# A four-layer transformer megakernel: rounding moved to GpSimd in the first attention, and the third attention's input rounded per batch inside its main part

## The chip, the cores and the metric

One NeuronCore of a Trainium2 chip runs the whole program in one launch. The metric is the device time of that launch in microseconds (us). On the core, TensorE (PE in the profile; PEld is its weight load) multiplies matrices into PSUM, VectorE (DVE), ScalarE (ACT) and GpSimd (POOL) work elementwise, and SyncE (SP) issues most DMAs. Each engine runs its own instruction list in order; engines wait for each other by semaphores.

## The reference

Activations `x` are 8 batches x 128 tokens x 256 features, the context has the same shape. Each of four layers computes `x = x + attention(layernorm(x), context)` and then `x = x + ffn(layernorm(x))`. The change touches two of the eight parts.

- **First attention (l0)**: 16 heads of 16 features over all 1024 context tokens. Queries, keys and values are rounded to 8 bits, `softmax(q k)` is rounded to 0..255 steps of its row maximum, then multiplied with the values.
- **Third attention (l2)**: the normalised input is scaled by `ln_w`, `ln_b`, divided by one of four per-feature input scales (for q, qx, k, v), clamped to +-448 and rounded to an 8-bit float (3 mantissa bits). Projections give 16 query heads, 16 cross query heads, 8 key heads and 8 value heads of 128 features, and cross keys and values from the context. Queries and keys are layer-normalised per head. Two attentions per batch (self and cross) follow; their outputs, side by side, are divided by `proj_smooth`, clamped and rounded in the same way, and projected back to 256 features by `wproj` (4096 x 256):

```
ln_out = _ln(hidden_states, ln_w, ln_b)
xq     = clip(ln_out / in_scale, -448, 448) -> bf16 -> fp8 e4m3 -> f32      (once per scale)
catq   = the same of concat(core, xout) / proj_smooth
out    = einsum('bsi,oi->bso', catq, wproj) * (proj_in_scale * proj_w_scale)
```

## The kernel before

The eight parts run one after the other, each a block of five engine programs written out by hand; the order of every engine's work is the order in the source.

**`attention_l0`, main part (profile lines 1797 to 1930).** 128 steps, one for each batch and head. In step `n` TensorE writes scores of 128 x 1024 into one of three PSUM buffers (L1817), VectorE takes the row maximum (`top`, L1901), GpSimd turns it into the bias of the exponential (L1807: one multiply-add on 128 x 1), ScalarE computes the exponential with its row sum and stores it as int16, which rounds it (`exps`, L1875), VectorE copies that to bf16 two steps later (`rounding`, L1907), and SyncE transposes it by DMA (L1798). Six steps behind, once in four steps, TensorE multiplies four heads with the values (`value`, L1830, 32 matmuls). Once per batch of 16 steps TensorE also turns the outputs (`turn_back`, `turn_output`) and multiplies them with the output weights (`output`). `score(n)` waits until the exponential of step `n - 3` has read its PSUM buffer.

**`attention_l2`.** It has two blocks.

The first (tiles `l2q_...`, L1256 to L1303) rounds the input for all 1024 tokens before anything else. ScalarE makes `lnT` (two instructions of 128 x 1024) and divides it (eight, L1281); VectorE clamps (L1303) and rounds each by `quantize` (L1220 to L1223: keep the exponent bits, bound the step, add 1.5 * 2^20 steps and take them away again), writing `xq`. Meanwhile SyncE loads `wproj` in 16 pieces into two buffers `wps`, and GpSimd copies each to bf16 (`keep`, L1288).

The second (tiles `l2x_...`, L1305 to L1567) walks over 16 items, two for each batch: side 0 (self) and side 1 (cross). An item has eight steps `t`. `phases(fn)` calls each engine's program with three items at once: `pi` is projected, `ai` (the one before) is in attention, `zi` (before that) finishes. `due(t, lag, ai, zi)` gives the group `a` of four heads (four groups per item) that stands `lag` steps after its start, `norm_due` the projected piece `u` (six per item). What matters here, per step:

- TensorE: projection `t` (L1417, six bf16 matmuls, or L1422), scores at even `t` (L1430), transposes of normalised pieces (L1437), transposes of the probabilities (L1444), values (L1451), and the output projection `y` (L1462) at lag 8.
- ScalarE: copies of the projection (`raw`, L1485), exponentials (L1490), `qT` and `kT` (L1499), `pT` (L1504), the read-out of the attention output into `of` (L1511).
- VectorE: statistics of piece `t` (L1536, `bn`), row maximum at even `t` (L1541), the normalisation of the piece three steps back (L1546, four instructions of 128 x 128), a reciprocal (L1552), and at even `t` clamp and `quantize` of `of` (L1559, L1220 to L1223).
- GpSimd: at `t` = 1, 3, 5 a chain of ten small instructions (L1386 to L1396) that makes the inverse deviations of two pieces, which VectorE's normalisations of steps `t + 2` and `t + 3` wait for; at even `t` the normalisation of the probabilities (L1400, `p_normed`), once VectorE's reciprocal is there.

`Chain.link` issues an instruction and waits for it on its own engine; `Chain.add` only counts it.

Of the kernel before, what the change touches and what calls it, by code (L numbers as in the profile page):

```python
# [1227 lines left out]
def attention_l2(pg, pre):  # L1232
# [8 lines left out]
    with outer:  # L1241
# [3 lines left out]
        xq = ob("xq", [P, 4, KD, T], BF16)  # L1245
        cols, scales = pre.tiles
        lnt, inverse, divided, steps, rounded, wp_kept = (
            pg.sem(f"l2q_{m}") for m in ("ln_affine", "inverse", "divided", "steps", "rounded", "wp_kept"))
        wp_in = [pg.sem(f"l2q_wp_in{i}") for i in range(2)]
        with ExitStack() as st:  # L1250
            def sb(m, shape, dt=F32):
                return st.enter_context(nc.sbuf_tensor(f"l2q_{m}", shape, dt))
            lnT = sb("lnT", [P, KD, T])
            rin = sb("rin", [P, 4 * KD])
            z = sb("z", [P, 2, T], BF16)
            step = sb("step", [P, 2, T], BF16)  # L1256
            wide = sb("wide", [P, 2, T])
            wps = sb("wps", [P, 2, 2, D])
            block = st.enter_context(nc.Block())
            jobs = [(k, j) for k in range(KD) for j in range(4)]  # L1260

            @block.sync
            def _(sp):
                for q in range(16):
                    if q >= 2:
                        sp.wait_ge(wp_kept, q - 1)
                    sp.dma_start(wps[:, q % 2], pg.dram["l2_wp"][:, 2 * q:2 * q + 2, :]).then_inc(wp_in[q % 2], 16)

            @block.scalar
            def _(act):  # L1270
                act.wait_ge(pre.arrived, 32)
                for k in range(KD):
                    nc.scalar.activation(lnT[:, k, :], pg.xnT[:, k, :], ACT.Identity, scale=cols[:, LNW + k:LNW + k + 1],
                                         bias=cols[:, LNB + k:LNB + k + 1]).then_inc(lnt, 1)
                act.wait_ge(inverse, 1)
                act.wait_ge(lnt, KD)
                for n, (k, j) in enumerate(jobs):
                    if n >= 2:
                        act.wait_ge(rounded, n - 1)
                    c = j * KD + k  # L1280
                    nc.scalar.activation(z[:, n % 2], lnT[:, k, :], ACT.Copy, scale=rin[:, c:c + 1]).then_inc(divided, 1)  # L1281

            @block.gpsimd
            def _(pool):

                def keep(q):
                    pool.wait_ge(wp_in[q % 2], 16 * (q // 2) + 16)
                    nc.gpsimd.tensor_copy(wp[:, 2 * q:2 * q + 2, :], wps[:, q % 2]).then_inc(wp_kept, 1)  # L1288
                for n in range(len(jobs)):
                    keep(2 * n)  # L1290
                    keep(2 * n + 1)

            @block.vector
            def _(dve):
                ch = Chain(dve, steps)
                dve.wait_ge(pre.arrived, 32)
                nc.vector.reciprocal(rin[:], cols[:, IN_SCALE:IN_SCALE + 4 * KD]).then_inc(inverse, 1)
                for n, (k, j) in enumerate(jobs):
                    u = n % 2
                    dve.wait_ge(divided, n + 1)  # L1300
                    if n >= 2:
                        dve.wait_ge(rounded, n - 1)
# [6 lines left out]
        with ExitStack() as st:  # L1309
# [3 lines left out]
            def psum(m, shape, dt=F32):  # L1313
                return st.enter_context(nc.psum_tensor(f"l2x_{m}", shape, dt))
# [1052 lines left out]
```

## Time and profile before

| | us |
|---|---|
| median of 3 runs | 1975.74 (1969.93 to 1977.56) |
| the profiled execution: its time | 1987.75 |
| its span | 1986.0 |
| busy: PE, DVE, ACT, POOL | 1622.9, 1170.6, 809.9, 616.7 |
| stage 79 to 302 (first attention, main part) | 223.0 |
| stage 932 to 972 (third attention, first block) | 40.0 |
| stage 972 to 1430 (third attention, main part) | 458.0 |

All times inside the kernel are from that one profiled execution, counted from the start of its span. A group line ends in busy time, mean ns of one instruction, and the idle time of the engine before them with what ended it. A timeline line has start, duration, engine, line and shapes; in square brackets stands how long the engine had been idle and for whom. An instruction that is blocked inside, for a port for example, shows as a longer duration, not as idle time.

### The profile page before, as it was taken

How to read it: one execution, taken by the hardware profiler on the slowest of the kernel's cores; microseconds unless marked ns; L12 is line 12 of the kernel's file. 1: busy time of each engine (PE TensorE's matmuls, PEld its weight loads, DVE VectorE, ACT ScalarE, POOL GpSimd, SP SyncE). 2: the span in 40 equal slices, each digit the busy share in tenths (PEclk: the TensorE clock that was granted, in tenths of full speed). 3: DMA queues.
4: the chain of work that ended last, by engine and by line, in shares of the span. 5: the costliest groups of instructions: out<-in, count | busy, mean ns of one | idle time of the engine just before them, and what ended most of it. 6: DMA issues, size and time to landing. Idle time of an engine off the chain costs nothing. (4 is left out here: it accounts for less than half of the span.)

```text
span 1986.0 us, 25201 instructions
## 1 busy us (share of the span) xinstructions
PE 1622.9 (82%) x8472; PEld 1004.9 (51%) x8472; DVE 1170.6 (59%) x2652; ACT 809.9 (41%) x1871; POOL 616.7 (31%) x980
## 2 busy tenths in 40 slices
PE   6688878999786899995389898898699989737762
PEld 5323234556454455554166666666555565535542
DVE  5799972223554632425789999999822255553225
ACT  3888773111322211112377777777621112412221
POOL 0022211000200197900455555655210000036662
PEclk9755558999687899998699999999889988768886
DMA  2288871110501213111100000000101100245535
GB/s 72 52 161 161 159 149 62 40 40 17 170 1 59 104 59 125 52 52 33 53 1 1 1 1 1 1 1 1 41 20 40 40 23 1 111 156 204 207 126 224
DMA packets 174224, 140.12 MB, mean 71 GB/s; under 512 B 141793, under 2 KB 154721, under 8 KB 170386
## 3 DMA queue, kind: packets, MB, share of 16 engines
q1 hardware_dynamic: 165314, 114.89, 20.6%
q0 software_dynamic: 6416, 22.03, 3.3%
q10 hardware_dynamic: 2368, 1.61, 0.3%
q8 instruction: 69, 1.13, 0.2%
q14 instruction: 57, 0.47, 0.1%
HBM read 85.43 MB, written 19.50 MB: 53 GB/s over the span
## 5 line engine op out<-in xcount | busy, mean ns | idle before, releaser
L1417 PE MATMUL l2x_pr<-l_w,l2x_xq 128*128 128x512 bf16 x576 | 141.1, 383 | 41.0 <-ACT credits L42 40.5
L350 PE MATMUL l1e_gu<-x_normT,l1e_w 128*128 128x512 f32 x384 | 170.8, 599 | 0.0
L1875 ACT ACTIVATE l0m_pf<-l0m_s,l0m_bias,l0x_sq 128x1024 int16<-128x1024 f32 x128 | 154.1, 1204 | 38.9 <-POOL l0m_bias L1807 38.9
L1901 DVE TENSOR_REDUCE l0m_mx<-l0m_s 128x1 f32<-128x1024 f32 x128 | 155.8, 1219 | 21.8 <-PE l0m_s L1817 20.3
L1817 PE MATMUL l0m_s<-l0x_kT,l0x_qT 48*128 48x512 bf16 x256 | 126.1, 620 | 35.9 <-ACT l0m_pf L1875 31.8
L350 PE MATMUL l0e_gu<-x_normT,l0e_w 128*128 128x512 f32 x272 | 121.5, 601 | 0.0
L1807 POOL TENSOR_SCALAR l0m_bias<-l0m_mx,l0x_nsq 128x1 f32<-128x1 f32 x128 | 46.7, 365 | 225.1 <-DVE l0m_mx L1901 222.3
L350 PEld LDWEIGHTS l1e_gu<-x_normT,l1e_w 128*128 128x128 f32 x384 | 73.8, 193 | 83.8 <-issue 82.8
L350 PE MATMUL l2e_gu<-x_normT,l2e_w 128*128 128x512 f32 x256 | 114.4, 602 | 0.0
L1546 DVE TENSOR_SCALAR l2x_raw<-l2x_raw,l2x_mv,l2x_rs 128x128 f32<-128x128 f32 x384 | 111.2, 351 | 3.5 <-POOL l2x_rs L1396 3.3
L1417 PEld LDWEIGHTS l2x_pr<-l_w,l2x_xq 128*128 128x128 bf16 x576 | 56.6, 99 | 96.3 <-ACT credits L42 40.7
L1400 POOL TENSOR_TENSOR x_norm<-x_norm,l2x_rsm 128x512 f32<-128x512 f32 x64 | 74.9, 1171 | 97.2 <-DVE l2x_rsm L1552 97.2
L426 DVE TENSOR_TENSOR l1e_h<-l1e_sil,l1e_gu 128x512 f32<-128x512 f32 x40 | 27.4, 687 | 131.4 <-ACT l1e_sil L402 131.4
L402 ACT ACTIVATE l1e_sil<-l1e_gu 128x512 f32<-128x512 f32 x48 | 28.6, 596 | 179.4 <-PE l1e_gu L350 179.4
L1536 DVE BATCH_NORM_STATS2 l2x_bn<-l2x_raw 128x6 f32<-128x128 f32 x384 | 82.5, 278 | 32.5 <-ACT l2x_raw L1485 32.4
L1437 PE MATMUL l2x_tr<-ident,l2x_raw 128*128 128x128 f32 x384 | 60.5, 280 | 44.6 <-DVE l2x_raw L1546 43.9
L1490 ACT ACTIVATE x_norm<-l2x_s,l2x_mx 128x128 f32<-128x128 f32 x256 | 90.3, 372 | 2.4 <-DVE l2x_mx L1541 2.4
L357 PE MATMUL l1e_y<-l1e_w,l1e_h 128*128 128x256 f32 x384 | 86.3, 379 | 0.6 <-DVE l1e_h L436 0.6
L426 DVE TENSOR_TENSOR l0e_h<-l0e_sil,l0e_gu 128x512 f32<-128x512 f32 x28 | 19.3, 688 | 110.7 <-ACT l0e_sil L402 110.7
L1396 POOL TENSOR_TENSOR l2x_rs<-l2x_rs,l2x_half 128x8 f32<-128x8 f32 x48 | 82.7, 1723 | 3.8
L350 PEld LDWEIGHTS l0e_gu<-x_normT,l0e_w 128*128 128x128 f32 x272 | 52.4, 193 | 60.0 <-issue 59.3
L357 PEld LDWEIGHTS l1e_y<-l1e_w,l1e_h 128*128 128x128 f32 x384 | 72.9, 190 | 19.4 <-issue 9.1
(515 smaller groups left out, 3636.8 us busy)
## 6 DMA issues: line engine op xcount, KB each, us to landing
l3m_w<-in_l_moe SPq DMA_DIRECT2D x16, 1280.0 KB
l1e_w<-in_l_ffn SPq DMA_DIRECT2D x24, 384.0 KB, 3.1
l_rows<-zero_row SPq DMA_DIRECT2D x8, 1024.0 KB, 11.1
l_w<-l_rows SPq DMA_DIRECT2D x8, 1024.0 KB, 11.8
l0e_w<-in_l_ffn SPq DMA_DIRECT2D x17, 384.0 KB, 3.0
l2e_w<-in_l_ffn SPq DMA_DIRECT2D x16, 384.0 KB, 3.1
ctx_tok<-l_route SPq DMA_DIRECT2D x8, 512.0 KB
l2q_wps<-in_l_wp SPq DMA_DIRECT2D x16, 256.0 KB, 2.7
```

The lines of the kernel that those rows point to most:

```text
L350: last = nc.tensor.matmul(gu[half][:, m, :], w[:, c % SW, (2 * k + m) * P:(2 * k + m + 1) * P], pg.xnT[:, k, cols(n)], start=(k == 0), sto ...
L357: last = nc.tensor.matmul(y[:, t, :], h[:, c % SH, t * P:(t + 1) * P], w[:, c % SW, WG:CHUNK], start=(c == 0 and t % 2 == 0), stop=False, ...
L1396: g.tensor_tensor(rs[:, 1, two, :], var, half[:, 0], ALU.pow).then_inc(s["rstd"], 1)
L1400: nc.gpsimd.tensor_tensor(p[:, a % 2], p[:, a % 2], rsm[:, a % 2].unsqueeze(2).to_broadcast([P, U, P]), ALU.mult).then_inc(s["p_normed"], 1)
L1417: last = nc.tensor.matmul(flat(pr[t % 2][:]), src[:, k, tokens], pg.l2_w3[:, part, k, at:at + W], start=(k == 0 and part == 0), stop=(k == ...
L1437: last = nc.tensor.transpose(tr[:, j, :], raw[:, u, j, :], pg.ident[:])
L1490: last = nc.scalar.activation(p[:, a % 2, j, :], s_ps[a % 2][:, j, :], ACT.Exp, bias=mx[:, a % 2, j:j + 1], accum_out=sm[:, a % 2, j:j + 1])
L1536: last = nc.vector.bn_stats(bn[:, t, j, :], raw[:, t, j, :])
L1546: last = nc.vector.tensor_scalar(raw[:, u, j, :], raw[:, u, j, :], mv[:, u, j, 0:1], rs[:, 1, u, j:j + 1], ALU.subtract, ALU.mult)
L1817: last = nc.tensor.matmul(s_ps[n % 3][:, g * HALF:(g + 1) * HALF], qT[:, h, b * P:(b + 1) * P], kT[:, h, g * HALF:(g + 1) * HALF], start=T ...
L1875: nc.scalar.activation(pf[:, n % 4, :], s_ps[n % 3][:], ACT.Exp, scale=sq[:, b, h:h + 1], bias=bias[:, n % 4:n % 4 + 1], accum_out=sm[:, b ...
L1901: nc.vector.tensor_reduce(mx[:, n % 4:n % 4 + 1], s_ps[n % 3][:], AX, ALU.max).then_inc(s["maxed"], 1)
```

## The change

In `attention_l0` GpSimd and VectorE trade two instructions: VectorE makes the bias right behind the maximum (on 128 x 1, after waiting for its own reduction), and GpSimd copies int16 to bf16 (128 x 1024).

In `attention_l2` the first block is gone. `lnT` is kept for the whole part; `xq` holds two batches. Batch 0 is rounded ahead of the main part (four ScalarE instructions of 128 x 128 and one VectorE chain of five instructions on 128 x 512, twice), batch `b + 1` during the two items of batch `b`. The `wproj` pieces are kept in the steps of the first two items, through one buffer. `quantize` loses its last instruction: `widen` ends in the f32 sum, and for `of` the subtraction is GpSimd's at lag 7, with two added waits of GpSimd; `y` moves from lag 8 to lag 9, and `cq` has three buffers. The upper bound of the step (256) goes; 1.5 * 2^20 is multiplied in its place.

```diff
-def quantize(nc, ch, z, step, wide, out):
+def widen(nc, ch, z, step, wide):
     v = nc.vector
     ch.link(v.tensor_scalar(step.bitcast(I16), z.bitcast(I16), 0x7F80, None, ALU.bitwise_and))
-    ch.link(v.tensor_scalar(step, step, 2.0 ** -6, 256.0, ALU.max, ALU.min))
-    ch.link(v.scalar_tensor_tensor(out=wide, in0=step, scalar=1.5 * 2.0 ** 20, in1=z, op0=ALU.mult, op1=ALU.add))
-    return v.scalar_tensor_tensor(out=out, in0=step, scalar=-1.5 * 2.0 ** 20, in1=wide, op0=ALU.mult, op1=ALU.add)
+    ch.link(v.tensor_scalar(step, step, 2.0 ** -6, 1.5 * 2.0 ** 20, ALU.max, ALU.mult))
+    return v.tensor_tensor(wide, step, z, ALU.add)
...
+            @block.sync
+            def _(sp):
+                for q in range(16):
+                    if q >= 1:
+                        sp.wait_ge(wp_kept, q)
+                    sp.dma_start(wps[:], pg.dram["l2_wp"][:, 2 * q:2 * q + 2, :]).then_inc(wp_in, 16)
...
             @block.gpsimd
...
+                def keep(q):
+                    pool.wait_ge(wp_in, 16 * q + 16)
+                    nc.gpsimd.tensor_copy(wp[:, 2 * q:2 * q + 2, :], wps[:]).then_inc(wp_kept, 1)
...
                     for t in range(8):
+                        if job := due(t, 7, ai, zi):
+                            _, a, m = job
+                            pool.wait_ge(s["widened"], m + 3)
+                            if ahead := norm_due(t, 3, pi, ai):
+                                pool.wait_ge(s["normed"], ahead[2] + 1)
+                            nc.gpsimd.tensor_tensor(cq[:, m % 3], wide[:, a % 2], step[:, a % 2], ALU.subtract).then_inc(s["quanted"], 1)
                         if pi is not None and t in (1, 3, 5):
...
                         if job := due(t, 2, ai, zi):
                             _, a, m = job
                             pool.wait_ge(s["recip"], m + 1)
+                            if ahead := due(t, 6, ai, zi):
+                                pool.wait_ge(s["widened"], ahead[2] + 3)
                             nc.gpsimd.tensor_tensor(p[:, a % 2], p[:, a % 2], rsm[:, a % 2].unsqueeze(2).to_broadcast([P, U, P]),
                                                     ALU.mult).then_inc(s["p_normed"], 1)
+                        if pi is not None and pi[0] == 0:
+                            keep(8 * pi[1] + t)
...
             @block.tensor
...
+                            pe.wait_ge(rounded, 2 * pi[0] + 2)
...
-                        if job := due(t, 8, ai, zi):
+                        if job := due(t, 9, ai, zi):
...
                             if side == 0 and a == 0:
+                                pe.wait_ge(wp_kept, 16)
...
             @block.scalar
...
+                def divide(b, half):
+                    act.wait_ge(rounded, 2 * b + half)
+                    for j in range(2):
+                        for k in range(KD):
+                            c = (2 * half + j) * KD + k
+                            nc.scalar.activation(xz[:, j, k, :], lnT[:, k, b * P:(b + 1) * P], ACT.Copy, scale=rin[:, c:c + 1]).then_inc(divided, 1)
...
+                            if t == 1 and pi[0] + 1 < B:
+                                divide(pi[0] + 1, side)
...
             @block.vector
...
+                def clamped(b, half):
+                    ch = xchain(b, half, 0)
+                    dve.wait_ge(divided, 2 * KD * (2 * b + half + 1))
+                    ch.link(nc.vector.tensor_scalar(xz[:], xz[:], 448.0, -448.0, ALU.min, ALU.max))
+                    ch.link(nc.vector.tensor_scalar(xstep[:].bitcast(I16), xz[:].bitcast(I16), 0x7F80, None, ALU.bitwise_and))
+                    ch.add(nc.vector.tensor_scalar(xstep[:], xstep[:], 2.0 ** -6, 1.5 * 2.0 ** 20, ALU.max, ALU.mult))
+
+                def stepped(b, half):
...
+                    ch.add(nc.vector.tensor_tensor(xwide[:], xstep[:], xz[:], ALU.add))
+
+                def narrowed(b, half):
...
+                    nc.vector.tensor_tensor(xq[:, b % 2, 2 * half:2 * half + 2], xwide[:], xstep[:], ALU.subtract).then_inc(rounded, 1)
...
                     for t in range(8):
...
+                        if pi is not None and pi[0] + 1 < B:
+                            if t == 3:
+                                clamped(pi[0] + 1, pi[1])
+                            if t == 5:
+                                stepped(pi[0] + 1, pi[1])
+                            if t == 7:
+                                narrowed(pi[0] + 1, pi[1])
...
@@ -1800,12 +1830,10 @@
             def _(pool):
                 for n in range(N):
-                    b, h = divmod(n, H)
-                    pool.wait_ge(s["maxed"], n + 1)
-                    if n >= 4:
-                        pool.wait_ge(s["exped"], n - 3)
-                    nc.gpsimd.tensor_scalar(bias[:, n % 4:n % 4 + 1], mx[:, n % 4:n % 4 + 1], nsq[:, b, h:h + 1], float(np.log(255.0)),
-                                            ALU.mult, ALU.add).then_inc(s["biased"], 1)
+                    pool.wait_ge(s["exped"], n + 1)
+                    if n >= 8:
+                        pool.wait_ge(moved[n % 8], 16 * (n // 8))
+                    nc.gpsimd.tensor_copy(pi[:, n % 8, :], pf[:, n % 4, :]).then_inc(s["rounded"], 1)
...
                     nc.vector.tensor_reduce(mx[:, n % 4:n % 4 + 1], s_ps[n % 3][:], AX, ALU.max).then_inc(s["maxed"], 1)
-
-                def rounding(n):
...
+                    dve.wait_ge(s["maxed"], n + 1)
+                    if n >= 4:
+                        dve.wait_ge(s["exped"], n - 3)
+                    nc.vector.tensor_scalar(bias[:, n % 4:n % 4 + 1], mx[:, n % 4:n % 4 + 1], nsq[:, b, h:h + 1], float(np.log(255.0)),
+                                            ALU.mult, ALU.add).then_inc(s["biased"], 1)
```

## Rows read from the trace of the kernel before

**Rows 1.** Windows view: stretch, busy of each engine, clock, DMA share, GB/s.
```profile
972.00:1430.00 458.00, 404.09 (x2368) 281.85 (x2368) 410.68 (x1231) 337.38 (x1062) 246.87 (x548) 1.00 0.00 1
```

**Rows 2.** Timeline, first attention: start, duration, engine, line.
```profile
119.82 1.23 DVE L1901 TENSOR_REDUCE l0m_mx<-l0m_s 128x1 f32<-128x1024 f32 x1 [0.47 <-PE l0m_s L1817]
121.14 0.37 POOL L1807 TENSOR_SCALAR l0m_bias<-l0m_mx,l0x_nsq 128x1 f32<-128x1 f32 x1 [2.36 <-DVE l0m_mx L1901]
121.55 1.20 ACT L1875 ACTIVATE l0m_pf<-l0m_s,l0m_bias,l0x_sq 128x1024 int16<-128x1024 f32 x1 [1.43 <-POOL l0m_bias L1807]
...
131.33 1.23 DVE L1901 TENSOR_REDUCE l0m_mx<-l0m_s 128x1 f32<-128x1024 f32 x1 [0.32 <-PE l0m_s L1817]
...
132.95 1.20 ACT L1875 ACTIVATE l0m_pf<-l0m_s,l0m_bias,l0x_sq 128x1024 int16<-128x1024 f32 x1 [0.47 <-POOL l0m_bias L1807]
...
134.30 1.03 PE L1817 MATMUL l0m_s<-l0x_kT,l0x_qT 48*128 48x512 bf16 x2 [0.21 <-ACT l0m_pf L1875]
...
137.30 1.04 PE L1830 MATMUL l0m_o<-l0m_pT,l0x_v 128*32 128x128 bf16 x32
138.28 2.02 PE L1817 MATMUL l0m_s<-l0x_kT,l0x_qT 48*128 48x512 bf16 x4
139.35 1.23 DVE L1901 TENSOR_REDUCE l0m_mx<-l0m_s 128x1 f32<-128x1024 f32 x1
...
157.99 1.23 DVE L1901 TENSOR_REDUCE l0m_mx<-l0m_s 128x1 f32<-128x1024 f32 x1 [0.32 <-PE l0m_s L1817]
```

**Rows 3.** Tile views: durations min/median/max in ns, first and last start.
```profile
L1907 DVE CAST l0m_pi<-l0m_pf x128: 412/416/427, 83.3 to 291.0; 128x1024 bf16<-128x1024 int16 x128
L74 POOL CAST l_w<-l_raw x36: 1037/1038/1456, 700.8 to 844.9; 128x1024 bf16<-128x1024 f32 x36
```

**Rows 4.** Timeline, second attention: a tiny VectorE instruction beside a GpSimd one.
```profile
506.88 3.52 POOL L781 MEMSET l1x_vz<- 128x4096 f32 x1
506.97 3.44 DVE L879 TENSOR_SCALAR l1x_own<-l1x_quarter 128x2 f32<-128x2 f32 x1 [2.97 <-POOL l1x_nm L780]
```

**Rows 5.** Tile views, the block that goes, and the first main instruction.
```profile
L1281 ACT ACTIVATE l2q_z<-l2q_lnT,l2q_rin x8: 1133/1148/1149, 934.9 to 964.1; 128x1024 bf16<-128x1024 f32 x8
L1288 POOL CAST l2x_wp<-l2q_wps x16: 616/676/1597, 935.2 to 962.3; 128x512 bf16<-128x512 f32 x16
...
DMA to landing us min/median/max: 2.5/2.7/3.5
...
972.13 0.13 PEld L1417 LDWEIGHTS l2x_pr<-l_w,l2x_xq 128*128 128x128 bf16 x2 [40.75 <-ACT credits L42]
```

**Rows 6.** Tile views, third attention's main part: durations.
```profile
L1220 DVE TENSOR_SCALAR l2x_step<-l2x_z x64: 293/294/1014, 1012.4 to 1426.9; 128x512 int16<-128x512 int16 x64
L1223 DVE SCALAR_TENSOR_TENSOR l2x_cq<-l2x_step,ctx_tok x64: 691/692/1411, 1014.5 to 1428.2; 128x512 bf16<-128x512 bf16 x64
L1400 POOL TENSOR_TENSOR x_norm<-x_norm,l2x_rsm x64: 1035/1132/1378, 1001.6 to 1420.5; 128x512 f32<-128x512 f32 x64
```

**Rows 7.** Timeline, third attention: starts of items, then one link of its loop.
```profile
1023.77 0.21 POOL L1386 TENSOR_TENSOR l2x_rs<-l2x_bn 128x8 f32<-128x8 f32 x1 [2.79 <-DVE l2x_bn L1536]
...
1155.74 0.87 DVE L1536 BATCH_NORM_STATS2 l2x_bn<-l2x_raw 128x6 f32<-128x128 f32 x4 [1.35 <-ACT l2x_raw L1485]
...
1180.74 1.10 DVE L1546 TENSOR_SCALAR l2x_raw<-l2x_raw,l2x_mv,l2x_rs 128x128 f32<-128x128 f32 x4
...
1183.62 0.87 DVE L1536 BATCH_NORM_STATS2 l2x_bn<-l2x_raw 128x6 f32<-128x128 f32 x4 [1.38 <-ACT l2x_raw L1485]
...
1192.66 2.09 POOL L1396 TENSOR_TENSOR l2x_rs<-l2x_rs,l2x_half 128x8 f32<-128x8 f32 x1
1194.72 1.04 POOL L1400 TENSOR_TENSOR x_norm<-x_norm,l2x_rsm 128x512 f32<-128x512 f32 x1
1194.79 1.82 DVE L1546 TENSOR_SCALAR l2x_raw<-l2x_raw,l2x_mv,l2x_rs 128x128 f32<-128x128 f32 x4
...
1197.94 1.64 POOL L1396 TENSOR_TENSOR l2x_rs<-l2x_rs,l2x_half 128x8 f32<-128x8 f32 x1
```

More of the change, by code:

```diff
@@ L1244, in attention_l2 @@
         wp = ob("wp", [P, 32, D], BF16)
-        xq = ob("xq", [P, 4, KD, T], BF16)
+        lnT = ob("lnT", [P, KD, T])
+        xq = ob("xq", [P, 2, 4, KD, P], BF16)
         cols, scales = pre.tiles
-        lnt, inverse, divided, steps, rounded, wp_kept = (
+        lnt, inverse, divided, xsteps, rounded, wp_kept = (
             pg.sem(f"l2q_{m}") for m in ("ln_affine", "inverse", "divided", "steps", "rounded", "wp_kept"))
[L1249 to L1302, printed above, removed]
-                    ch.link(nc.vector.tensor_scalar(z[:, u], z[:, u], 448.0, -448.0, ALU.min, ALU.max))
-                    quantize(nc, ch, z[:, u], step[:, u], wide[:, u], xq[:, j, k, :]).then_inc(rounded, 1)
@@ L1412, in fn @@
                             if side == 0 or 2 <= t < 6:
-                                src = xq[:, (K_, K_, Q_, Q_, Q_, Q_, V_, V_)[t] if side == 0 else QX]
+                                src = xq[:, pi[0] % 2, (K_, K_, Q_, Q_, Q_, Q_, V_, V_)[t] if side == 0 else QX]
                                 at = t * W if side == 0 else 4096 + (t - 2) * W
@@ L1461, in fn @@
                                 first, final = side == 0 and a == 0 and j == 0, side == 1 and a == 3 and j == U - 1
-                                last = nc.tensor.matmul(y[:, 0:D], cq[:, a % 2, j, :], wp[:, side * 16 + a * U + j, :], start=first, stop=final)
+                                last = nc.tensor.matmul(y[:, 0:D], cq[:, m % 3, j, :], wp[:, side * 16 + a * U + j, :], start=first, stop=final)
                             if side == 1 and a == 3:
@@ L1518, in _, with xchain @@
                 pg.credit(nc.vector, s["quanted"], 2)
+                pg.credit(nc.vector, s["widened"], 2)
+                XSTEPS = 4
+                def xchain(b, half, n):
+                    ch = Chain(dve, xsteps)
+                    ch.base, ch.n = (2 * b + half) * XSTEPS, n
+                    return ch
+                def clamped(b, half):
[5 more added lines that the diff above has]
+                def stepped(b, half):
+                    ch = xchain(b, half, 3)
+                    ch.wait()
+                    ch.add(nc.vector.tensor_tensor(xwide[:], xstep[:], xz[:], ALU.add))
+                def narrowed(b, half):
+                    xchain(b, half, XSTEPS).wait()
+                    if b >= 2:
+                        dve.wait_ge(s["proj"], 16 * (b - 1))
+                    nc.vector.tensor_tensor(xq[:, b % 2, 2 * half:2 * half + 2], xwide[:], xstep[:], ALU.subtract).then_inc(rounded, 1)
+                dve.wait_ge(pre.arrived, 32)
+                nc.vector.reciprocal(rin[:], cols[:, IN_SCALE:IN_SCALE + 4 * KD]).then_inc(inverse, 1)
+                for half in range(2):
+                    clamped(0, half)
+                    stepped(0, half)
+                    narrowed(0, half)
                 for c in range(4):
@@ L1897, in top @@
                 def top(n):
+                    b, h = divmod(n, H)
                     dve.wait_ge(s["scores"], n + 1)
```

44 lines of the change are left out of this document (29 added, 15 removed).

## The prediction

> **What bounds the kernel now.** I read the stages first (windows view and tiles' first and last starts), because the parts run one after another and only two of them change. Outside them nothing moves, so everything below is about 223 us of the first attention's main part, the 40 us block of the third attention and its main part of 458 us [rows 1].
>
> In the first attention the timeline shows what ends each wait. A loop runs over three steps: an exponential starts at 132.95, the scores that take its buffer start at 134.30 (1.35 later); scores at 138.28 give a maximum at 139.35 (1.07); a maximum at 119.82 gives the bias at 121.14 (1.32) and the exponential at 121.55 (0.41) [rows 2]. Sum 4.15, or 1.38 a step. TensorE inserts work into it in order: the value matmuls push the next scores by 0.98 (137.30 to 138.28), once in four steps. One scores-pair costs TensorE 0.83 more of its own, so four steps cost 4.15 + 0.98 + 0.83 = 5.96, and a batch of 16 four of those plus the turns and the output projection. Maxima 16 steps apart stand 26.66 apart (131.33 and 157.99) [rows 2]. VectorE (1.22 for the maximum, 0.42 for the copy, overlapping to 1.47 a step) is right behind it [rows 2, 3].
>
> In the third attention's main part VectorE is busy 410.7 of 458 us, TensorE 404.1, ScalarE 337.4, GpSimd 246.9, at full granted clock [rows 1]; an item takes 27.9 us (1155.74 to 1183.62) [rows 7]. VectorE's durations spread: the same mask instruction takes 0.29 or 1.01, the last rounding step 0.69 or 1.41; GpSimd's p_normed takes 1.04 to 1.38 [rows 6]. And when p_normed (1194.72, 1.04) starts right after a chain, the four normalisations behind that chain take 1.82 instead of 1.10 [rows 7]. So a wide GpSimd instruction and most VectorE instructions exclude each other, and one of them waits for the whole of the other.
>
> **The change, part by part (in terms of the profiled execution).**
>
> *First attention.* The bias moves to VectorE. No row shows it on 128 x 1 there; I take 0.17 (a lower end of 0.1 and an upper one of 0.37, GpSimd's own row). Maximum to exponential falls from 1.73 to about 1.5, the loop by 0.23. VectorE per step: 1.22 + 0.03 + 0.09 = 1.34, below 1.47, so it does not take over. A batch holds four loop passages: 4 x 0.23 = 0.92 us, 8 batches: 7.4; I take -8. The copy on GpSimd is bounded by its cast of 128 x 1024 (f32 to bf16) with 1.04 to 1.46 [rows 3]; the source here is int16. At 1.04 it fits into a step of 1.6 and ends earlier than VectorE's did, which came two steps late. At 1.46 it still fits.
> The trace speaks against this part in one place: a VectorE tensor_scalar of 128 x 2 stood 3.44 us beside a GpSimd memset of 3.52 [rows 4]. If 128 x 1 behaves like it, the bias can wait up to a whole copy (1.04). It fits between two copies while ScalarE runs without a gap; after each delay of TensorE by 0.2 to 1.2 it does not, and is put off until the copy ends. That is some five times in a batch, 2.8 us, less the 0.9 won: +15 over 8 batches (a range of 0 to +30). The Trainium skill, "Vector Engine (DVE) Microarchitecture Reference", section 5.1 (Performance modes), lets a one-source instruction take both ports, the second of them shared with GpSimd, when its outermost dimension above one is even, or odd and equal in source and destination. The row with two elements agrees; whether one element on each side counts as odd and equal (the +15) or as no such dimension at all (the -8) the page leaves open, and no row here shows it.
>
> *First block of the third attention: removed.* Projections began at 972.13 [rows 5], the block at 932. Now: lnT of batch 0 (0.6), four divisions (1.2, from 1.15 for 128 x 1024), one VectorE chain 0.3 + 0.33 + 0.33 + 0.65 + 0.7, then the second four and the chain again, since `divide(0, 1)` waits for `rounded`: about 9 us. Projections from 941: -31.
>
> *`keep` in the first two items.* One buffer: copy (0.62), issue, landing (2.7) [rows 5] is 3.4 us per piece, and GpSimd waits for it in order, with the chains and p_normed behind. A pair of steps with a chain costs 3.9 (chain) + 0.62 + 2.8 + 0.62 = 8.0, as one landing is hidden by the chain and the other is not; the pair without chain 6.9. Laid out from 941 the first chain of item 2 starts at 1007.9 instead of 1023.77 [rows 7]. So of the 31 us 16 remain; bounds: landing 2.5 gives 18, copies of 1.6 beside VectorE 8. SyncE's queue holds nothing else. TensorE's first y waits for all 16 pieces; the last is kept at 1004.9, before that y is due (step 1 of item 2), so this wait costs nothing.
>
> *Items 2 to 13.* VectorE loses per group one 0.69 instruction (4 per item, -2.9), gains per item 0.3 + 0.33 + 0.33 + 0.65 + 0.65 = 2.3. GpSimd gains four subtractions, with mixed inputs about 1.05 as p_normed [rows 6]. ScalarE gains four small divisions (1.2), inside its idle quarter. By busy time all have room. But VectorE and GpSimd now pass work to and fro. From the end of the chain of `t` = 1 (time 0):
> - p_normed follows at once and blocks the normalisation of `t` = 3, which ends at 1.85 (1194.75 to 1196.61 in rows 7). The clamp of `clamped` takes the port next (2.15), then the subtraction (3.2), which the mask waits for. Chain of `t` = 3, 3.85 long: 7.05.
> - VectorE: mask and bound 3.8, statistics, maximum, normalisation, reciprocal 6.3, clamp and widen 1.75: 8.05. Only then p_normed of `t` = 4 (added wait): 9.15. Normalisation of `t` = 5: 10.1; `stepped` 10.8; subtraction 11.9; chain of `t` = 5: 15.8. p_normed of `t` = 6 follows at once and blocks the normalisation of `t` = 7: 17.6.
> - From there into a side 1: `narrowed` 0.65, statistics 0.8, maximum 0.6, normalisation 1.0, reciprocal 0.1, widen 1.75, p_normed 1.1, subtraction 1.05, chain 3.95: 11.0. Into a side 0 the projection has to wait for `narrowed`, then 1.4 + 0.7 until the statistics: 13.1.
> Two items: 2 x 17.6 + 11.0 + 13.1 = 59.3, or 29.65 each, against 27.8: +1.85, over 12 items +22. If every exclusion falls well (0.8 less at `t` = 3 and at `t` = 7, no clamp between) it is 27.8: 0; if the chains are slowed to 4.5 by VectorE's instructions, 31.3: +42. I take +22. TensorE (25 us of work per item) and the y matmuls, a step later with a third buffer, are covered by it; uncovered, TensorE's end of an item would not fall below 25.
>
> *The last two items and the drain.* No input rounding; groups cost VectorE 2.4 instead of 3.1 to 3.8, and ScalarE (3.2 a group) comes next; one subtraction more at the very end: -5.
>
> Sum: -8 - 31 + 15 + 22 - 5 = -7 (the 16 above is 31 - 15). The profiled execution took 1987.75, 12 above the median; I carry the difference to the median: 1975.7 - 6 = 1970.
>
> **Rivals.**
> A. *GpSimd's steps fall between VectorE's as placed, and the item stays at 27.8 or falls a little.* For: VectorE's blocked time in the rows (0.7 on one of its instructions in most groups) is about 2 us an item, and the added waits aim at just that. Against: the path above counts GpSimd at 20.5 us of work per item plus 9 of waits. Time: 1970 - 22 = 1948.
> B. *The bias instruction waits for GpSimd's copy.* It decides once a bias is issued while a copy runs. For: rows 4. Against: one element. -8 becomes +15: 1970 + 23 = 1993, slower.
> C. *The loop between VectorE and GpSimd costs more*, because VectorE's instructions also hold up the chain's small ones: +3.5 an item, 1970 + 20 = 1990, slower. For: one chain's last instruction took 2.09, another's 1.64 [rows 7].
> D. *The copy on GpSimd does not do what the cast row says*: int16 input above 1.6 us makes GpSimd the bound of 128 steps; at 2.0 it is +45: 2020. Against: both rows of casts and their even spread.
>
> **How the numbers follow.** Forecast 0.36, A 0.32, B 0.18, C 0.10, D 0.04. Half a per cent is 10 us, about what a measurement can tell. The forecast's own range is 1958 to 1982, with 0.07 of its chance below 1966 and 0.03 above 1985.6. A is faster but for 0.01; B, C and D are slower but for 0.01. Faster 0.07 + 0.31 = 0.38, same 0.26 + 0.02 = 0.28, slower 0.03 + 0.31 = 0.34. The range 1938 to 1996 leaves out D, the lower edge of A and the upper edges of B and C, some 2 in 10.
>
> **What would show it.** First attention: maxima 16 steps apart 25.7 instead of 26.66, the bias on VectorE near 0.17 (B: a spread up to 1.2), GpSimd's copy near 1.04. First projection near 941. Item 2's first chain near 1008, with GpSimd idle for the `wps` DMAs some 30 us in all. Items 29.7 us apart (A: 27 to 28; C: above 31), the normalisation behind the chains of `t` = 1 and `t` = 5 at 1.8. GpSimd waiting for VectorE's widened, normed about 9 us an item. The prediction is wrong if items are shorter than 28.5, if the keeps do not stretch items 0 and 1, or if the copy is above 1.5.

## The result, and where the time went

The changed kernel took 2007.74 us (median of 4 runs, 2004.56 to 2008.85) against 1976.65 us before (4 runs, 1969.93 to 1979.67): a ratio of 1.0175, 95% interval [1.0151, 1.0199], so it is slower by 1.5 to 2%. 1970 had been forecast, and a range up to 1996.

The profiled execution has a span of 2006.8 us, against 1986.0 before. This difference of 20.8 understates the 31 us between the medians: the last expert part, which is the same code in both, took 271.2 us in the profile of before and 258.9 in the one of after. So stages are compared and not spans. The first attention's main part went from 223.2 to 217.1 us. The third attention, from its first instruction to its last y matmul, ended 1429.6 us into the span before and 1464.6 after: +35.0, of which the table gives the parts (starts of items are the first statistics of each; items are numbered from 0, and items with an odd number are side 1).

| third attention, us | before | after | difference |
|---|---|---|---|
| start of item 2 | 1017.2 | 1001.75 | -15.45 |
| items 2 to 13, mean of one | 27.73 | 31.43 | +3.70 (x 12 = +44.4) |
| start of item 14 to the last y matmul | 79.7 | 85.7 | +6.0 |

Counted from the first instruction of the third attention (932.36 before, 930.90 after) item 2 starts 14.0 earlier; 1.5 of the -15.45 belongs to what stands ahead of that part.

The first attention behaves as the loop of [rows 2] said. Timeline of the changed kernel, the same place (start, duration, engine, line):

```profile
134.20 1.23 DVE L1930 TENSOR_REDUCE l0m_mx<-l0m_s 128x1 f32<-128x1024 f32 x1
...
135.12 1.04 POOL L1836 CAST l0m_pi<-l0m_pf 128x1024 bf16<-128x1024 int16 x1 [0.87 <-ACT l0m_pf L1903]
135.46 0.21 DVE L1934 TENSOR_SCALAR l0m_bias<-l0m_mx,l0x_nsq 128x1 f32<-128x1 f32 x1
...
135.71 1.20 ACT L1903 ACTIVATE l0m_pf<-l0m_s,l0m_bias,l0x_sq 128x1024 int16<-128x1024 f32 x1 [0.65 <-DVE l0m_bias L1934]
```

Its tile views (min/median/max in ns) answer to [rows 3] and [rows 4]:

```profile
L1934 DVE TENSOR_SCALAR l0m_bias<-l0m_mx,l0x_nsq x128: 212/214/215, 83.7 to 286.0; 128x1 f32<-128x1 f32 x128
...
L1836 POOL CAST l0m_pi<-l0m_pf x128: 1037/1042/1045, 85.3 to 287.6; 128x1024 bf16<-128x1024 int16 x128
```

From the start of the maximum to the exponential it is 1.51 us (1.73 before), and the bias of 135.46 runs in the middle of a copy. The spread is what one reads in the tile views: 212 to 215 ns in all 128 cases, of which 29 lie wholly inside a copy; and no copy takes more than 1045. An instruction that had waited for the other engine would show it as length, as the 3.44 us of [rows 4] did. Maxima 16 steps apart stand 25.88 us apart in most batches, where 26.66 was the figure before.

The start of the third attention came as worked out. Timeline and tile view of the changed kernel; the first row answers to 972.13 in [rows 5], the second is the staged copy, the third the DMA it waits for:

```profile
940.16 0.13 PEld L1384 LDWEIGHTS l2x_pr<-l_w,l2x_xq 128*128 128x128 bf16 x2 [10.39 <-DVE l2x_xq L1534]
```

```profile
L1326 POOL CAST l2x_wp<-l2x_wps x16: 603/612/734, 933.7 to 1002.4; 128x512 bf16<-128x512 f32 x16
its engine sat idle before it (us, times) until:
  DMA l2x_wps<-in_l_wp: 23.4, 10
```

The loss is in the items. The stage's windows row against [rows 1] says first what it is not: VectorE's busy time fell from 410.7 to 396.1 us, and yet the stage is longer. TensorE is busy 425.9 of 525, at a granted clock of 0.96.

```profile
940.00:1465.00 525.00, 425.93 (x2330) 290.08 (x2368) 396.11 (x1237) 361.00 (x1113) 328.35 (x623) 0.96 0.03 8
```

The groups of the page name the waits (busy, mean ns | idle before, and what ended it):

```profile
L1384 PE MATMUL l2x_pr<-l_w,l2x_xq 128*128 128x512 bf16 x538 | 140.4, 398 | 39.8 <-DVE l2x_xq L1534 36.4
...
L1558 DVE BATCH_NORM_STATS2 l2x_bn<-l2x_raw 128x6 f32<-128x128 f32 x384 | 83.1, 278 | 73.6 <-ACT l2x_raw L1474 73.6
...
L1364 POOL TENSOR_TENSOR x_norm<-x_norm,l2x_rsm 128x512 f32<-128x512 f32 x64 | 66.6, 1041 | 103.7 <-DVE ctx_tok L1218 103.7
```

TensorE now waits 36.4 us for `xq`, the rounded input, eight times: 10.39 at the start of the part, and seven times 3.15 to 3.93 where a new batch begins (26 together). VectorE's statistics wait 73.6 us for the raw projections that come late behind that (32.4 before). GpSimd's normalisation waits 103.7 us for VectorE's `widen`, a wait that the change put there; but before it had stood idle at the same place for 97.2 us, for VectorE's reciprocal, so its idle time alone does not tell what the new wait costs. One passage from a side 1 into a side 0 shows how the first comes about (timeline of the changed kernel):

```profile
1119.49 1.64 POOL L1358 TENSOR_TENSOR l2x_rs<-l2x_rs,l2x_half 128x8 f32<-128x8 f32 x1
...
1121.09 1.04 POOL L1364 TENSOR_TENSOR x_norm<-x_norm,l2x_rsm 128x512 f32<-128x512 f32 x1
1121.16 1.82 DVE L1568 TENSOR_SCALAR l2x_raw<-l2x_raw,l2x_mv,l2x_rs 128x128 f32<-128x128 f32 x4 [1.81 <-POOL l2x_rs L1358]
1122.91 0.68 DVE L1534 TENSOR_TENSOR l2x_xq<-l2x_xwide,l2x_xstep 128x512 bf16<-128x512 f32 x1
...
1123.64 0.98 PEld L1384 LDWEIGHTS l2x_pr<-l_w,l2x_xq 128*128 128x128 bf16 x6 [3.81 <-DVE l2x_xq L1534]
1123.87 1.24 PE L1384 MATMUL l2x_pr<-l_w,l2x_xq 128*128 128x512 bf16 x5 [3.76 <-DVE l2x_xq L1534]
...
1125.15 0.69 ACT L1474 ACTIVATE l2x_raw<-l2x_pr,l2c_scales 128x512 f32<-128x512 f32 x1 [3.04 <-PE l2x_pr L1384]
...
1125.87 0.87 DVE L1558 BATCH_NORM_STATS2 l2x_bn<-l2x_raw 128x6 f32<-128x128 f32 x4 [1.89 <-ACT l2x_raw L1474]
```

`narrowed` stands last in VectorE's item, behind a normalisation that waits for GpSimd's chain and then for GpSimd's p_normed (1.82 instead of 1.10). TensorE's first projection of the next batch asks for it: TensorE stands still for 3.76 us, and being in order it does none of its other work meanwhile.

The stop has a second price, in TensorE's clock. Two pairs of items of the changed kernel (items 5 and 6, items 9 and 10):

```profile
1093.78:1155.54 61.76, 50.63 (x293) 34.64 (x297) 49.39 (x156) 45.32 (x140) 40.20 (x77) 1.00 0.01 1
1218.92:1283.55 64.63, 53.14 (x293) 36.72 (x297) 49.58 (x156) 45.33 (x140) 40.19 (x77) 0.95 0.00 1
```

At five of the seven stops (those that end at 998.70, 1185.61, 1249.17, 1313.81 and 1376.72) the granted clock falls to the lower of its two levels, 1.2 GHz, within 1.5 us of the stop's end; at the two that end at 1062.11 and 1123.87 it does not. The pairs of items without a low stretch take 61.75 us each, and items 2 to 13 take 377.2 where six such pairs would take 370.5. Some 6 of these 6.7 us lie in items 7 to 13, which have the low stretches: about 0.5 an item.

### The profile page after: what moved, and what is told of

Same layout as the page of the kernel before. It is cut to its first block and busy times, and to the rows that moved or that the text cites. A ratio compares the mean times of both kernels' runs of the same rounds, so it can differ in the third digit from the quotient of the medians.

```text
span 2006.8 us, 25491 instructions
## 1 busy us (share of the span) xinstructions
PE 1640.5 (82%) x8434; PEld 1012.7 (50%) x8472; DVE 1109.7 (55%) x2629; ACT 828.9 (41%) x1929; POOL 771.1 (38%) x1044
## 5 line engine op out<-in xcount | busy, mean ns | idle before, releaser
L1836 POOL CAST l0m_pi<-l0m_pf 128x1024 bf16<-128x1024 int16 x128 | 133.4, 1042 | 137.0 <-ACT l0m_pf L1903 136.1
L1384 PE MATMUL l2x_pr<-l_w,l2x_xq 128*128 128x512 bf16 x538 | 140.4, 398 | 39.8 <-DVE l2x_xq L1534 36.4
L1568 DVE TENSOR_SCALAR l2x_raw<-l2x_raw,l2x_mv,l2x_rs 128x128 f32<-128x128 f32 x384 | 130.4, 399 | 35.9 <-POOL l2x_rs L1358 35.9
L1558 DVE BATCH_NORM_STATS2 l2x_bn<-l2x_raw 128x6 f32<-128x128 f32 x384 | 83.1, 278 | 73.6 <-ACT l2x_raw L1474 73.6
L1404 PE MATMUL l2x_tr<-ident,l2x_raw 128*128 128x128 f32 x384 | 65.4, 296 | 58.4 <-DVE l2x_raw L1568 58.4
L1364 POOL TENSOR_TENSOR x_norm<-x_norm,l2x_rsm 128x512 f32<-128x512 f32 x64 | 66.6, 1041 | 103.7 <-DVE ctx_tok L1218 103.7
L1339 POOL TENSOR_TENSOR l2x_cq<-ctx_tok,l2x_step 128x512 bf16<-128x512 f32 x64 | 81.9, 1280 | 45.2 <-DVE l2x_raw L1568 41.8
L1404 PEld LDWEIGHTS l2x_tr<-ident,l2x_raw 128*128 128x128 f32 x384 | 46.2, 149 | 89.0 <-DVE l2x_raw L1568 85.1
```

Of the source, the lines that this page charges most:

```text
L1339: nc.gpsimd.tensor_tensor(cq[:, m % 3], wide[:, a % 2], step[:, a % 2], ALU.subtract).then_inc(s["quanted"], 1)
L1384: last = nc.tensor.matmul(flat(pr[t % 2][:]), src[:, k, :], pg.l2_w3[:, part, k, at:at + W], start=(k == 0 and part == 0), stop=(k == KD - ...
L1404: last = nc.tensor.transpose(tr[:, j, :], raw[:, u, j, :], pg.ident[:])
L1558: last = nc.vector.bn_stats(bn[:, t, j, :], raw[:, t, j, :])
L1568: last = nc.vector.tensor_scalar(raw[:, u, j, :], raw[:, u, j, :], mv[:, u, j, 0:1], rs[:, 1, u, j:j + 1], ALU.subtract, ALU.mult)
L1836: nc.gpsimd.tensor_copy(pi[:, n % 8, :], pf[:, n % 4, :]).then_inc(s["rounded"], 1)
```

## The experiments

Three theories stood at the start. H: passing work to and fro between VectorE and GpSimd costs what the item gained. W: the two waits that place GpSimd's wide steps cost it. X: the rounding of the input inside the items costs it. Where a run's ratio is given, it is to the kernel before on the same chip. The changed kernel, the runs up to no_x, the next four and the last four were timed in separate groups, so ratios are compared between groups and not times; each ratio is known to 0.0015 to 0.003, 3 to 6 us.

**l0_only.** The kernel before with the first attention's trade alone (lines 1807 and 1907 of before: bias to VectorE, copy to GpSimd).

> The kernel before with the first attention's trade alone (bias on VectorE, copy on GpSimd). The two traces show batches of 25.88 instead of 26.66 us, the bias at 0.21 us without a spread and the copy at 1.04, so this should give -5 to -6 us: 1971. If the trade has side effects on the parts behind it, or the trace's 6 us is the chance of one execution, it is 0.

Ratio 0.9962 [0.9947, 0.9978], 1981.43 us on a chip where before took 1988.81; first attention 216.2 us, items of the third 27.70. So the trade is a gain of some 7 us, in the size of the prediction's -8 and a little over the 5 to 6 expected here, and the loss sits elsewhere.

**no_waits.**

```diff
-                            if ahead := norm_due(t, 3, pi, ai):
-                                pool.wait_ge(s["normed"], ahead[2] + 1)
...
-                            if ahead := due(t, 6, ai, zi):
-                                pool.wait_ge(s["widened"], ahead[2] + 3)
```

> The changed kernel without the two added waits of GpSimd that only place its wide steps (normed before the subtraction, widened before p_normed). Theory W, the placing waits themselves are the cost: items fall from 31.5 to about 28.5 us, 2008 - 40 = 1968. Theory H, the hand-over between VectorE and GpSimd costs it with or without the placing, since either engine then waits for the port: VectorE's blocked instructions come back (some 0.7 us per group), items 30.5 to 31, about -10: 1998. Theory X, the input rounding inside the items is the cost: no change, 2005 to 2008.

Ratio 1.0065 [1.0045, 1.0085]; items 30.60, and the tail behind item 14 80.6 instead of 85.7. W is worth 0.011, about 22 us, by the timed ratios, and 14 us by the profiles of the part; the 40 us expected if W were all are missed, so that is not all.

**sub_dve.** As no_waits, and the subtraction is VectorE's again, right behind `widen`:

```diff
-                            nc.gpsimd.tensor_tensor(cq[:, m % 3], wide[:, a % 2], step[:, a % 2], ALU.subtract).then_inc(s["quanted"], 1)
...
+                            nc.vector.tensor_tensor(cq[:, m % 3], wide[:, a % 2], step[:, a % 2], ALU.subtract).then_inc(s["quanted"], 1)
```

> The changed kernel with the subtraction of the outputs back on VectorE behind widen (0.69 us each, four an item) and without the placing waits; the input rounding stays in the items. H: GpSimd is light again, the loop through it is gone; VectorE has the 27.7 of before plus 2.3 of input rounding: items of 29 to 30 us, 1975 to 1985. W: like the kernel without waits or slightly slower. X: stays at 31 or more, 2005.

Ratio 1.0117 [1.0086, 1.0149]; items 31.18, 0.6 more than in no_waits. H falls: the 29 to 30 that it expected are missed, and GpSimd's subtraction is a gain here. The gate does not hide the answer, since TensorE's stop there is 2.53 us in this run and 2.66 in no_waits. split_nw_ld below says the same: there the work is still passed to and fro, and the items are only 0.42 longer than before.

**no_x.** The input of batches 1 to 7 isn't rounded; TensorE reads batch 0's.

```diff
-                            pe.wait_ge(rounded, 2 * pi[0] + 2)
+                            pe.wait_ge(rounded, 2)
...
-                                divide(pi[0] + 1, side)
...
-                                clamped(pi[0] + 1, pi[1])
...
-                                stepped(pi[0] + 1, pi[1])
...
-                                narrowed(pi[0] + 1, pi[1])
```

> The changed kernel with the input rounding of batches 1 to 7 left out (they use batch 0's rounded input, so the output of those batches is not the reference's); GpSimd's subtraction and both waits stay. X: items fall to 27.7 or below, 2008 - 50 = 1958. H: the loop between VectorE and GpSimd stays, without the clamp and mask at t = 3 (-1.8) and narrowed at t = 7 (-0.7, and -1.5 where a side 0 follows): items of 28.5 to 29, 1970. W: 29 to 30, 1980.

Ratio 0.9927 [0.9904, 0.9951]; items 28.16. X is the main cause: 3.3 of the 3.7 us an item hang on it, though both placing waits are in. (From item 3 on the granted clock is 1.00 in this run, so the clock's 0.5 an item is in the 3.3.) A second reading matters as much. Windows view of this kernel's stage, as [rows 1]:

```profile
937.00:1418.00 481.00, 417.78 (x2368) 285.05 (x2365) 370.33 (x1159) 339.43 (x1057) 332.84 (x623) 0.98 0.03 9
```

VectorE is busy 40 us less than in [rows 1], some 2.5 an item, and the item is not shorter than before's 27.73. The placing waits are still in this run. If they cost here what they cost in split_nw (0.9 an item), the item without them would be about 27.3, an estimate: at most 0.5 us won for 2.5 us of VectorE's time. So VectorE's busy time was hardly what set the item of before.

X itself can work in three ways, which the next four runs are to separate: G, TensorE waits for `xq`; S, ScalarE's four divides (1.27 us together) hold up the exponentials and the next raw copy; D, VectorE's added work stretches the chain.

**late_divide.** `divide` moved from behind the raw copy of `t` = 1 to the end of `t` = 2.

> The changed kernel, but ScalarE's four divides of the next batch stand at the end of t = 2 of an item, behind the raw copies of the second group and the copy of the attention's output, and not between raw and exp at t = 1 (4 x 0.39 = 1.6 us an item). Run with three others (early_narrow, ungated, no_divide) that split the 3.4 us an item which leaving the rounding out gave back. Theory S (ScalarE's divides hold up exp and the second raw, which the normalising chain waits for): items at 31.5 - 1.5 = 30.0 us, ratio to before about 1.008. Theory G (TensorE's projection of the next batch waits for the rounded input): the divides come later, so the gate opens no earlier; 31.5 or more, ratio 1.017 to 1.022. Theory D (VectorE's and GpSimd's own added work stretches the chain): no change, 1.017.

Ratio 1.0123 [1.01, 1.0145]; items 30.62.

**no_divide.** `divide` left out after batch 0.

> ScalarE's divides of batches 1 to 7 left out, everything else as in the changed kernel: VectorE rounds what batch 0's divides left. Theory S: items at 31.5 - 1.6 = 29.9, ratio 1.007. Theory G: little, since narrowing stays at its place: 1.015. Theory D (work on VectorE and GpSimd): 1.017. Against late_divide it tells whether moving the divides gives all that removing them gives.

Ratio 1.0131 [1.0102, 1.016]; items 30.60. Moving the divides gives just what leaving them out gives: 0.8 us an item. It is their place that costs, not their time. S holds, but for a minor part (30.0 and 29.9 had been expected if it were all). In both runs TensorE still stops at the gate, 3.52 us per batch, and late_divide's odd items 3 to 13 have clocks of 0.95 or 0.96, so the 0.8 is not measured at full clock.

**early_narrow.**

```diff
-                            if t == 7:
+                            if t == 6:
                                 narrowed(pi[0] + 1, pi[1])
```

> The changed kernel, but VectorE's narrowing of the rounded input stands at t = 6 and not at t = 7. Theory G: TensorE's idle in front of the projection's first transposes (36 us of 39.8 in the changed kernel) falls by up to 4.5 us for eight items: ratio down by 0.010 to 0.018, to 1.000 to 1.008. Theory S: nothing or little, 1.015 to 1.018. Theory D: 1.017, or worse by the 0.68 us of the narrowing now in front of the last reading of the chain.

Ratio 1.0056 [1.0038, 1.0074]; items 29.87. One line moved by one step gives back 0.012. TensorE's stop is 0.82 us at the first new batch and at most 0.24 at the later ones, and the granted clock is 1.00 in items 2 to 13. G is the main part.

**ungated.** All rounding is done (its results for batches 1 to 7 all go to the second buffer); TensorE reads batch 0's and waits for no later one:

```diff
-                            pe.wait_ge(rounded, 2 * pi[0] + 2)
+                            pe.wait_ge(rounded, 2)
...
-                                src = xq[:, pi[0] % 2, (K_, K_, Q_, Q_, Q_, Q_, V_, V_)[t] if side == 0 else QX]
+                                src = xq[:, 0, (K_, K_, Q_, Q_, Q_, Q_, V_, V_)[t] if side == 0 else QX]
```

> All the rounding of the input is done, at its places, but TensorE always reads batch 0's rounded input and waits for no later one; the projections of batches 1 to 7 thus come from batch 0's rows. Theory G: nearly all of the 3.4 us an item comes back, items at 28.3, ratio about 0.995. Theory S: the divides still hold up the second raw; items at 31, ratio 1.015. Theory D: no change, 1.017. If it lands between (items at 29.9), the gate is worth what comes back and the work the rest.

Ratio 1.0035 [1.0021, 1.005]; items 29.57, between the 28.3 expected if G were all and the 31 expected if S were. The gate is worth 0.014, its effect on the clock included; what is left against no_x (28.16) is 1.4 an item for the work itself.

This suggests a repair. K and Q, needed at once, do not have to wait for V and for side 1's Q: round them as the first half, an item earlier.

**split_gate.**

```diff
-                            pe.wait_ge(rounded, 2 * pi[0] + 2)
+                            pe.wait_ge(rounded, 2 * pi[0] + (1 if side == 0 and t < 6 else 2))
...
-                            c = (2 * half + j) * KD + k
+                            c = (half + 2 * j) * KD + k
...
-                    nc.vector.tensor_tensor(xq[:, b % 2, 2 * half:2 * half + 2], xwide[:], xstep[:], ALU.subtract).then_inc(rounded, 1)
+                    nc.vector.tensor_tensor(xq[:, b % 2, half::2], xwide[:], xstep[:], ALU.subtract).then_inc(rounded, 1)
```

> The changed kernel, but the input is rounded in another pairing: the first half is the one that K and Q read, the second the one that QX and V read, and TensorE waits at side 0's first six projections for the first half alone, which is narrowed an item earlier. Nothing else is moved. Theory G (what early_narrow and ungated point to: TensorE waits for the half narrowed at the end of the item before): items like ungated's, 29.5 us, ratio 1.002 to 1.005. If the delay came from VectorE's added work in front of the chain's small ones and not from the gate: 1.012 to 1.018.

Ratio 1.0032 [1.0013, 1.005]; items 29.64, as in ungated. The whole cost of the gate was an order of data, at no cost in work. The granted clock is 1.00 from item 2 to item 13. Items 5 and 6 take 58.99 us together, against 61.76 in the changed kernel at the same clock: the stop itself is worth 1.4 an item, and the clock's 0.5 comes on top in the items that had it. The first projection also needs one half only: it comes 5.5 us after the part's first instruction and not 9.3.

**split_nw.** split_gate and no_waits together.

> split_gate without the two waits that place GpSimd's subtraction and normalisation behind VectorE's. If the gate's and the waits' costs add (0.014 and 0.011 of the time): ratio 0.992. If the waits cost only because they delayed the gate: no better than split_gate, 1.003. Items at 28.6 us if they add, 29.5 if not.

Ratio 0.9926 [0.9903, 0.9949], 1955.56 us against 1969.32; items 28.73, tail 80.0. The two costs add. Here the waits are worth 0.0106 by the timed ratios and 16 us (0.008) by the profiles. The same passage as above, timeline of this kernel:

```profile
1103.34 1.41 POOL L1360 TENSOR_TENSOR x_norm<-x_norm,l2x_rsm 128x512 f32<-128x512 f32 x1
...
1103.77 2.69 DVE L1564 TENSOR_SCALAR l2x_raw<-l2x_raw,l2x_mv,l2x_rs 128x128 f32<-128x128 f32 x4
...
1104.18 1.07 PEld L1380 LDWEIGHTS l2x_pr<-l_w,l2x_xq 128*128 128x128 bf16 x6
...
1104.29 1.46 PE L1380 MATMUL l2x_pr<-l_w,l2x_xq 128*128 128x512 bf16 x6
...
1104.72 1.15 POOL L1337 TENSOR_TENSOR l2x_cq<-ctx_tok,l2x_step 128x512 bf16<-128x512 f32 x1
```

The normalisation takes 2.69 us here, behind both wide GpSimd steps, against 1.82 in the changed kernel: the exclusion is worse. But TensorE's projection starts without a wait, 2.1 us before VectorE writes the other half of `xq`. The page's groups:

```profile
L1380 PE MATMUL l2x_pr<-l_w,l2x_xq 128*128 128x512 bf16 x576 | 143.4, 387 | 7.7 <-DVE l2x_xq L1530 6.3
...
L1360 POOL TENSOR_TENSOR x_norm<-x_norm,l2x_rsm 128x512 f32<-128x512 f32 x64 | 77.5, 1210 | 56.4 <-DVE l2x_rsm L1570 55.6
```

p_normed takes 1210 ns on average without its placing wait and 1041 with it (in split_gate as in the changed kernel); and the kernel with the shorter one is the slower. Which of the instructions behind p_normed pays for the wait was not separated.

**split_nw_ld.** split_nw with late_divide.

> split_nw with ScalarE's divides at the end of t = 2. In late_divide this gave 0.8 us an item, but the gate was closed there. Theory S (the divides hold up exp and raw): another 0.5 to 0.8 us an item, ratio 0.003 to 0.005 below split_nw's. If in late_divide it worked through the gate only: nothing.

Ratio 0.9925 [0.9902, 0.9948], 1954.06 us. In the profile the items are 28.15 (0.58 less; it is the odd ones that shrink, from 29.28 to 28.18) and the stage ends 6.7 us sooner counted from its start; the timed ratio moves by 0.0001. The last part of that profiled execution is 5.4 us longer than in split_nw's (259.8 and 254.4), in unchanged code. Whether the divides' place still brings anything stays open: 6.7 us would be 0.0034, and each ratio is known to 0.0023.

**split_nw_shift.** split_nw with the rounding late in the item: `divide` at the end of `t` = 4, `clamped` at 6, `stepped` and `narrowed` at 7.

> split_nw with all rounding of the input late in the item, now that the gate leaves a whole item of room: divides at the end of t = 4, clamp and mask at t = 6, sum and narrowing at t = 7. What the input's rounding still costs in split_nw is VectorE's and ScalarE's work in front of the normalising chain (raw, statistics, chain, norm at t = 2 to 6). If so: items at 28.2, ratio 0.985 to 0.990. If it is contention with GpSimd wherever the work stands: like split_nw.

Ratio 0.9933 [0.9908, 0.9958]; items 28.49. The place costs or gives 0.24 an item; the timing cannot tell it from split_nw, and the 0.985 to 0.990 hoped for were missed. Little is left to be had by moving this work.

The three split_nw versions (0.9925 to 0.9933) beat the kernel before and the changed one; l0_only (0.9962, another chip, intervals that touch) is the simple second. In the profiles the third attention, from its first instruction to its last y matmul, takes 497.2 us before, 533.7 changed and 489.1 in split_nw: the block's removal pays only there, with 8 us, and the first attention's 6 make up the rest of split_nw's gain of 14.

## Why the prediction was wrong, point by point

| step | forecast | shown |
|---|---|---|
| first attention, bias and copy traded | -8 | -6.1 in the profile; -7.4 timed (l0_only) |
| first projection | 941 | 940.2 |
| chain of item 2 (1023.77 before) | 1007.9 | 1008.3 |
| start of item 2 | -16 | -15.45, of which -14.0 in this part |
| items 2 to 13 | +22 (29.65 each) | +44.4 (31.43 each) |
| last items and drain | -5 | +6.0 |

The failed step is "Items 2 to 13", a term of the right sign and half the measured size, and with it the last items, of the wrong sign. Together they are 33 us off, about the distance of the forecast to the result (38). (The sum itself is -7 and was carried over to the median as -6; that slip is 1 us.) What the runs put in their place:

- *"Into a side 0 the projection has to wait for `narrowed`"* was in the sum with 2.1 us per two items (13.1 against 11.0). Opening the gate gave 1.79 an item, 3.6 per two. Of it the stop is 1.4 an item at full clock, 2.8 per two where 2.1 had been put. The lowered clock is the other 0.5 an item, and the prediction had no term for it. In the rows above TensorE's stop is 3.76 us, and what it would have done in it comes late too: VectorE was laid out for its own path, TensorE's queue behind the wait was not. "TensorE (25 us of work per item)" was held to be covered, by its busy time.
- *The placing waits* were put down at VectorE's and GpSimd's readiness (p_normed of `t` = 4 put off from 7.05, the end of GpSimd's chain, to 8.05, the end of VectorE's widen). They cost 0.91 an item (29.64 to 28.73) and 5.3 in the tail (85.3 to 80.0). That is half of the last items' error of 11 us. Without the waits the tail is 80.0 against 79.7 before: item 14 is 0.9 shorter, what follows it 1.3 longer, and why the 5 us of gain did not come stays open.
- *"ScalarE gains four small divisions (1.2), inside its idle quarter"*: 0.58 to 0.8 an item in the profiles, by place and not by time. They stood between the raw copy of `t` = 1 and the exponentials. The 0.58 is what split_nw_ld shows with the gate open; its timed ratio does not confirm it.
- These three are 1.79 + 0.91 + 0.58 = 3.28 of the 3.70 an item, taken away in this order. The remaining 0.42 (28.15 against 27.73) is the balance of the rounding that came in and the instruction that VectorE gave away; it was not split further.
- *"So of the 31 us 16 remain"* was right to 2 us (14.0 in this part), in part by luck: in the first two items the sum had neither a stop at the gate (3.15 us at 998.70) nor the granted clock of 0.85 and 0.81, where before had 1.00 in both. ungated and split_gate start item 2 after 67.8 and 64.4 us of the part, the changed kernel after 70.85.

The forecast read the exclusion of VectorE and GpSimd as the core of the item ("a wide GpSimd instruction and most VectorE instructions exclude each other"). The exclusion is real. The tile view of the new mask shows it where it was foreseen, behind the subtraction:

```profile
L1522 DVE TENSOR_SCALAR l2x_xstep<-l2x_xz x16: 294/1214/1217, 934.0 to 1360.0; 128x512 int16<-128x512 int16 x16
...
L1364 POOL TENSOR_TENSOR x_norm<-x_norm,l2x_rsm x64: 1035/1041/1043, 980.7 to 1455.6; 128x512 f32<-128x512 f32 x64
```

But it is no measure of the cost: the waits took it off p_normed entirely (1043 at most, [rows 6] had 1378), and the kernel was slower for it, by 0.011 as timed.

Of the rivals, C had the size of the items (+3.5 each, 1990) but another mechanism: it blamed the chain's small instructions. A fell with the items. B fell with the 212 to 215 ns of the bias. The page that it leaned on, the Trainium skill's "Vector Engine (DVE) Microarchitecture Reference", section 5.1, had left open whether one element per partition takes the second port; 29 such instructions lay inside a copy on GpSimd and none was held up by it, so in this case it does not contend. D fell with the copy's 1042.

The chances gave slower 0.34 and same 0.28, and the range ended at 1996. Two of the three sources of loss were in the text as named waits. Both were priced by when the two sides are ready, and not by what is queued behind the engine that stops.

## What to carry to other kernels

Price a wait by the engine that has to stop for it and by all that is queued behind, not by the two that hand over: 3.76 us of TensorE's stop came from a 0.68 us instruction that was merely last in VectorE's order, and the granted clock fell at most such stops. Before a producer is moved, ask which part of its result the consumer reads first, and produce that part first; splitting the gate cost no work and gave back 0.014. A wait that only places instructions so that they do not collide is worth trying without: here two engines in collision were faster than two engines in order.

## What the runs showed of the hardware

- A one-element VectorE tensor_scalar (128 x 1, f32) takes 212 to 215 ns and is not held up by a GpSimd copy of 1042 ns that runs beside it; the 128 x 2 of [rows 4], beside a memset, took 3.44 us. Whether the element count or the GpSimd instruction makes the difference was not separated.
- GpSimd's copy of 128 x 1024 from int16 to bf16 takes 1042 ns, as its cast from f32 [rows 3]; VectorE's took 416.
- GpSimd's subtraction with one f32 and one bf16 input and a bf16 output takes 1152 ns at least for 128 x 512, where its product of p_normed, all f32, takes 1035; "about 1.05" had been assumed for both. Operation, types and the broadcast operand of the product differ at once:

```profile
L1339 POOL TENSOR_TENSOR l2x_cq<-ctx_tok,l2x_step x64: 1152/1160/1482, 999.6 to 1462.4; 128x512 bf16<-128x512 f32 x64
```

- TensorE's granted clock fell to its lower level (1.2 GHz) at five of seven stops of 3.15 to 3.93 us in the changed kernel, and stayed at 1.00 in items 3 to 13 of ungated, early_narrow, split_gate and split_nw, where TensorE does not stop there. Over the whole part it is 0.96 in the changed kernel and 0.99 in split_nw; half of the low time lies in the first two items (0.85 and 0.81, against 0.92 and 0.89 in split_nw), where GpSimd waits for the pieces of `wproj`. A projection matmul takes 398 ns on average in the changed kernel, and 387 both in its items 2 to 13 and in the whole of split_nw.

```profile
937.00:1417.00 480.00, 412.06 (x2360) 280.53 (x2358) 424.64 (x1233) 355.82 (x1113) 330.08 (x623) 0.99 0.03 9
```
